# Mean squares of a gated norm on one NeuronCore: four transposes and a column sum in place of eight products with a column of ones

## The chip, the cores and the metric

One core of a Trainium2 chip runs the whole kernel in one launch. The metric is the device time in microseconds (us) of one execution. The engines are PE (TensorE), whose weight loads are listed apart as PEld, DVE (VectorE), ACT (ScalarE), POOL (GpSimd) and SP (SyncE), which issues the transfers.

## What is computed

Input x has 32 sequences of 64 tokens with 512 features, 2048 tokens in all. Three sublayers are added to it in turn, each on the layer norm of what came before: a state space layer, an attention of 32 heads over a small context, and a mixture of four low-rank experts. Nearly all of the time is in the first, which in short is:

```
proj = input_states @ in_proj_w.T           # gate 8192, x 8192, B and C 1024 each, dt 128
xBC  = silu(conv(xBC) + conv_b)             # 4 taps, causal, per channel
y    = _ssd(hs, A, Bm, Cm, D, dt, dt_bias)  # decayed attention inside each sequence
g    = y * silu(gate)
gg   = g.reshape(b, l, G, GS)               # G = 8 groups of GS = 1024 channels
var  = mean(gg * gg, axis=-1)               # one number for each token and group
g    = gg * rsqrt(var + EPS) * norm_w
out  = g @ out_w.T
```

The change concerns `var`: for each token, the mean of 1024 squares.

## The kernel before

The tokens are cut into 4 blocks of 512 (`TB`) and the channels into 8 groups. An iteration is one block and one group, 32 iterations in all (`number(tb, g)`), and their loops are unrolled. Each engine has its own list of instructions, written out by hand in the order in which it runs them. Semaphores join the lists: a `wait_ge` holds back everything behind it on its engine.

In an iteration channels lie on the partitions and the block's 512 tokens along the columns. A group's input weights are 18 units of 128 channels: B, C, and eight pairs X and G. Each unit is 12 products of 128x512 on PE (`unit`, into the PSUM banks `p_in`), since weights and activations are split in two parts of type fp32r and three combinations of the parts are added up. DVE and ACT run the convolution (`conv`). X tiles are transposed on PE (`to_tokens`: four transposes of 128x128, as products of `x_t` and the identity `id_sb`). The decayed attention is `heads`, products of 64x64 into the two PSUM banks of `p_y`. DVE multiplies with the gate (`gated`, the tile `g_f`). ACT rounds that to `g_hi` and squares it to `g_sq`, and POOL makes the rest `g_lo` and adds the squares of the eight channel tiles into `ss` (128 channels by 512 tokens, fp32). The output projection (`project`) adds 12 products for each channel tile into the four banks `p_out`.

`rsqrt(var + EPS)` is the same for all channels of a group, so it is applied after the projection: `accumulate` multiplies each `p_out` tile, in which tokens are on the partitions, with the column `rms`. For this the mean squares are wanted with the tokens on the partitions. `mean_squares` on PE does that: for each of the four token tiles, `ss` is the stationary operand and a column of ones the moving one, so that the product is the sum over channels, one column of `p_y[:, 1, :]`. Each such fp32 product runs as two weight loads and two matmuls, so a call has eight. DVE's `variance` scales the four columns and adds 1e-5 (`msv`), POOL's `inverse_rms` raises them to the power -0.5 (`rms`).

The place: the mean squares of iteration n - 1 are made in iteration n, behind its units 4 and 5 and in front of half of a projection:

```python
unit(5, tb, g, n)
mean_squares(n - 1)
project(CPG - 1, *back, range(0, 2))
slot(1, tb, g, n)
to_tokens(1, n)
```

`slot(1)` begins with PE's wait for `msv_done`, since PE is about to write `p_y` again (in some iterations at once, with four transposes of expert rows, `experts_in`, or of step sizes, `by_token`; in the others later). On DVE, `variance(n - 1)` stands behind the convolution of unit 4 and in front of `x_tokens(1)`, which waits for `to_tokens(1)`. On POOL, `inverse_rms(n - 1)` comes a little later, in front of `g_low(0, n)`.

The last iteration's mean squares are made behind the loop by code of their own, with ones.

Of the kernel before, what the change touches and what calls it, by code (L numbers as in the profile page):

```python
# [7 lines left out]
P = 128  # L8
# [6 lines left out]
CPG = INTER // GROUPS // P  # L15
# [3 lines left out]
QT = TB // P  # L19
ITERS = NTB * GROUPS  # L20
# [18 lines left out]
def decoder_kernel(nc, x, ctxv, amask, wt, wdt, owt, params, dtb, alog, ffa, ffb,  # L39
                   ident, c_mask, c_bd, c_v2, c_eq, out):  # L40
    F32, F32R = mybir.dt.float32, mybir.dt.float32r
    ACT, ALU, AX = mybir.ActivationFunctionType, mybir.AluOpType, mybir.AxisListType
# [7 lines left out]
    with outer:  # L50
        def alloc(stack):
            def sb(name, shape, dt=F32, align=None):
                wide = 4 * int(np.prod(shape[1:])) >= 256
                return stack.enter_context(nc.sbuf_tensor(name, shape, dt, align_bytes=align or (64 if wide else 32)))
            return sb

        def sem(name):
            return outer.enter_context(nc.semaphore(name))

        sb = alloc(outer)  # L60
        id_sb = sb("id_sb", [P, P])
        half_neg = sb("half_neg", [P, QT])
        ones = sb("ones", [P, 1])
# [7 lines left out]
        dpar = sb("dpar", [P, CPG])  # L71
        dts = sb("dts", [P, QT, HPG])
        msv = sb("msv", [P, QT])
        rms = sb("rms", [P, QT])
        st6 = sb("st6", [P, QT, 6])
        mv = sb("mv", [P, QT, 2])
# [11 lines left out]
        p_y = outer.enter_context(nc.psum_tensor("p_y", [P, 2, 512], F32))  # L88
# [4 lines left out]
        sb = alloc(main)  # L93
# [4 lines left out]
        sb = alloc(loop)  # L98
# [16 lines left out]
        ss = sb("ss", [P, TB])  # L115
# [22 lines left out]
        sb = alloc(raw)  # L138
# [11 lines left out]
        sb = alloc(tail)  # L150
# [21 lines left out]
        s_done = sem("s_done"); tr_done = sem("tr_done"); xtok_done = sem("xtok_done")  # L172
        y_done = sem("y_done"); yread = sem("yread"); g_done = sem("g_done")
        sq_done = sem("sq_done"); ghi_done = sem("ghi_done"); glo_done = sem("glo_done"); ss_done = sem("ss_done")
        out_done = sem("out_done"); ms_done = sem("ms_done"); msv_done = sem("msv_done"); rms_done = sem("rms_done")
        dve_own = sem("dve_own"); act_own = sem("act_own"); tap_own = sem("tap_own"); ln_own = sem("ln_own")
        dif_first = sem("dif_first"); clamp_first = sem("clamp_first"); exp_first = sem("exp_first"); s_first = sem("s_first")
        first_in = [sem(f"first_in{h}") for h in range(2)]
# [63 lines left out]
        def waves(stage, places):  # L242

            turns = [(at, q, k) for k, ats in places.items() for q, at in enumerate(ats) if at is not None]
            for _, q, k in sorted(turns):
                y0, y1 = TAIL_BANKS[q]
                stage(k, q, LOOP_TILES + q, tail_tiles[q], y0, y1)
# [222 lines left out]
        def _(pe):  # L470
            def mm(o, l, r, first, last):
                return nc.tensor.matmul(o, lhsT=l, rhs=r, start=first, stop=last)  # L472
# [320 lines left out]
            def mean_squares(n):  # L793
                pe.wait_ge(ss_done, SUMS * (n + 1))
                pe.wait_ge(yread, CPG * (n + 1))
                pe.sem_inc(hold, 1)
                for h in range(QT):
                    tok = slice(h * P, (h + 1) * P)
                    ins = mm(p_y[:, 1, h:h + 1], ss[:, tok], ones[:, :], True, True)
                ins.then_inc(ms_done, 1)  # L800

            def body(tb, g):
# [14 lines left out]
                if begun:  # L817
                    state_products(n)
                    project(CPG - 2, *back)
                    to_tokens(0, n)  # L820

                    unit(4, tb, g, n)
# [5 lines that stand above are left out]
                else:  # L828
                    unit(4, tb, g, n)
                    unit(5, tb, g, n)  # L830
                    pe.wait_ge(dtr_done, 1)
                    by_token(0)
                    state_products(n)
                    to_tokens(0, n)
                    unit(6, tb, g, n, 1)
# [31 lines left out]
            for h in range(QT):  # L867
                tok = slice(h * P, (h + 1) * P)
                mm(p_y[:, 1, h:h + 1], ss[:, tok], ones[:, :], True, False)
                mm(p_y[:, 1, h:h + 1], g_sq[:, 0, tok], ones[:, :], False, False)  # L870
                ins = mm(p_y[:, 1, h:h + 1], g_sq[:, 1, tok], ones[:, :], False, True)
# [3 lines left out]
            c = CPG - 1  # L875
            pe.wait_ge(o_ld[c % RING_O], 16 * ((CPG // RING_O) * (ITERS - 1 - GROUPS) + c // RING_O + 1))
            pe.wait_ge(glo_done, CPG * ITERS)
            for h in range(QT):
                tok = slice(h * P, (h + 1) * P)
                for j, (ga, wo) in enumerate(((g_hi, 0), (g_hi, 1), (g_lo, 0))):  # L880
                    ins = mm(p_out[h][:, :], ga[:, c % 2, tok], o_ring[:, c % RING_O, wo, :], False, j == 2)
# [415 lines left out]
        def _(dve):  # L1297
            V = nc.vector
# [185 lines left out]
            def gated(c, n):  # L1484

                dve.wait_ge(yread, CPG * n + c + 1)
                dve.wait_ge(gate_done, CPG * n + c + 1)
                if c >= 2 or not first(n):
                    dve.wait_ge(sq_done, CPG * n + c - 1)
                    dve.wait_ge(glo_done, CPG * n + c - 1)  # L1490
                V.tensor_tensor(g_f[:, c % 2, :], t_y[:, c % 2, :], sg[:, (CPG * n + c) % GATES, :], ALU.mult).then_inc(g_done, 1)  # L1491

            def variance(n):
                dve.wait_ge(ms_done, n + 1)
                V.tensor_scalar(msv[:, :], p_y[:, 1, 0:QT], 1.0 / (CPG * P), 1e-5, ALU.mult, ALU.add).then_inc(msv_done, 1)

            def accumulate(tb, n):
# [184 lines left out]
            def body(tb, g):  # L1682
# [51 lines left out]
                for k in range(1 if begun else 2, CPG):  # L1734
# [8 lines left out]
                    if k == 1 and begun:  # L1743
                        variance(n - 1)
# [33 lines left out]
            for c in (CPG - 2, CPG - 1):  # L1778
                skipped(c, ITERS - 1)
                gated(c, ITERS - 1)  # L1780
            variance(ITERS - 1)

            def moments_and_mean(S, src):

# [288 lines left out]
```

## Time and profile before

| | us |
|---|---|
| median of 3 runs (2845.37 to 2847.9) | 2847.12 |
| the profiled execution's own time | 2843.42 |
| its span, from first to last instruction | 2841.6 |

| engine | busy us | share of the span |
|---|---|---|
| PE | 2804.8 | 99% |
| PEld | 2274.4 | 80% |
| DVE | 1990.1 | 70% |
| ACT | 1462.6 | 51% |
| POOL | 1315.5 | 46% |

The rows further down come from one profiled execution, whose time is 3.7 us below the median of the runs. Times in a row are us from the start of the span unless they are marked ns. A matmul's end is modelled, and matmuls overlap, so that the busy time of PE is no sum of costs: what a piece of PE work costs is read from the chain of work, or from one start to the next. The mean granted clock of TensorE over the span is 0.997 of full speed.

### The profile page before, as it was taken

The numbers are of one execution on the slowest core, as the hardware profiler recorded it, in microseconds if no ns is written. First come the engines' busy times: TensorE is split into PE (matmuls) and PEld (weight loads), VectorE is DVE, ScalarE is ACT, GpSimd is POOL, SyncE is SP. The second block draws the span as 40 slices with busy tenths as digits, with TensorE's granted clock in tenths as the row PEclk, the third lists the DMA queues.
The fourth block names the chain that finished last, engine by engine and source line by source line (L and its number), as shares of the span: only waits on it lengthen the run. The fifth ranks groups of instructions, "written<-read, shape, count | busy, mean of one in ns | idle before, by whom it ended". The sixth has DMA issues, their size and how long they took to land.

```text
span 2841.6 us, 56494 instructions
## 1 busy us (share of the span) xinstructions
PE 2804.8 (99%) x22298; PEld 2274.4 (80%) x22298; DVE 1990.1 (70%) x3152; ACT 1462.6 (51%) x2205; POOL 1315.5 (46%) x840
## 2 busy tenths in 40 slices
PE   7999999999999999999999999999999999999998
PEld 5788888878788788887888888888888888878886
DVE  8777768887667757677676766677666666666767
ACT  5666656655445545445445454544545444453545
POOL 4766767775344333443343443424434334343334
PEclk9999999999999999999999999999999999999999
DMA  7788777778565555565665665555656656555530
GB/s 253 274 298 300 264 270 258 269 257 291 181 200 189 181 183 182 181 192 182 203 193 180 200 189 174 186 180 185 203 180 192 193 173 203 181 184 187 186 130 31
DMA packets 179428, 578.27 MB, mean 203 GB/s; under 512 B 25248, under 2 KB 31904, under 8 KB 171104
## 3 DMA queue, kind: packets, MB, share of 16 engines
q1 hardware_dynamic: 179168, 574.66, 61.5%
q8 instruction: 180, 2.95, 0.4%
q14 instruction: 80, 0.66, 0.1%
HBM read 460.29 MB, written 114.29 MB: 202 GB/s over the span
## 4 chain that ended last, share of the span: by engine, by line
PE 91%; DVE 6%; ACT 1%; issue 1%; DMA 0%; POOL 0%; SPq 0%; DVEq 0%; ACTq 0%; POOLq 0%
PE p_in L472 53%; PE p_out L472 23%; PE p_y L472 9%; PE p_in L562 4%; DVE cv L1430 1%; PE p_y L700 1%; DVE o_ring L1370 1%; DVE t_y L1479 0%; DVE g_f L1491 0%; DVE mx L1600 0%; ACT cv L942 0%; DVE sc L1587 0%; DVE cum L1392 0%; DMA raw_w<-wt 0%; DVE decay L1462 0%
## 5 line engine op out<-in xcount | busy, mean ns | idle before, releaser
L472 PE MATMUL p_in<-xnb,w_ring 128*128 128x512 f32 x6864 | 1673.2, 396 | 1.8 <-DVE cv L1430 0.9
L472 PEld LDWEIGHTS p_in<-xnb,w_ring 128*128 128x128 f32 x6864 | 1260.8, 188 | 262.6 <-issue 2.7
L1430 DVE SCALAR_TENSOR_TENSOR cv<-p_in,cpar,cv 128x504 f32<-128x504 f32 x954 | 699.8, 734 | 469.2 <-ACT cv L942 445.4
L1856 POOL TENSOR_TENSOR g_lo<-g_f,g_hi 128x512 fp32r<-128x512 f32 x256 | 338.1, 1322 | 1195.8 <-ACT g_hi L942 1195.8
L472 PE MATMUL p_out<-o_ring,g_hi 128*128 128x512 f32 x2048 | 638.3, 393 | 1.7 <-POOL g_lo L1856 1.7
L942 ACT ACTIVATE cv<-p_in,cpar 128x512 f32<-128x512 f32 x318 | 246.6, 775 | 636.9 <-PE p_in L472 600.5
L472 PEld LDWEIGHTS p_out<-o_ring,g_hi 128*128 128x128 f32 x2048 | 379.4, 188 | 80.3 <-issue 2.3
L472 PE MATMUL p_out<-o_ring,g_lo 128*128 128x512 f32 x1024 | 399.6, 390 | 0.0
L1467 DVE TENSOR_TENSOR x_tok<-p_in,dts 128x512 f32<-128x512 f32 x256 | 176.5, 689 | 285.7 <-PE p_in L562 284.0
L942 ACT ACTIVATE x_t<-cv 128x512 f32<-128x512 f32 x256 | 160.9, 628 | 309.9 <-DVE t_y L1479 285.9
L1867 POOL TENSOR_TENSOR ss<-ss,g_sq 128x512 f32<-128x512 f32 x190 | 310.3, 1633 | 7.4
L1911 POOL TENSOR_TENSOR decay<-decay,cumk 128x2048 f32<-128x2048 f32 x63 | 234.8, 3727 | 38.9 <-DMA decay<-cum_scr 37.7
L942 ACT ACT_TABLE_LOAD x183 | 234.8, 1283 | 4.0 <-PEq L2067 0.7
L1848 POOL TENSOR_TENSOR w_ring<-raw_w,w_ring 128x512 fp32r<-128x512 f32 x144 | 209.2, 1477 | 51.5 <-ACT w_ring L942 35.8
L942 ACT ACTIVATE sg<-p_in 128x512 f32<-128x512 f32 x254 | 149.3, 588 | 160.9 <-PE p_in L472 160.9
L472 PEld LDWEIGHTS p_out<-o_ring,g_lo 128*128 128x128 f32 x1024 | 192.2, 188 | 40.7
L1479 DVE SCALAR_TENSOR_TENSOR t_y<-x_t,dpar,p_y 128x256 f32<-128x256 f32 x512 | 210.9, 474 | 1.1 <-PE p_y L472 1.1
L1491 DVE TENSOR_TENSOR g_f<-t_y,sg 128x512 f32<-128x512 f32 x256 | 180.2, 744 | 0.1
L942 ACT ACTIVATE g_hi<-g_f 128x512 fp32r<-128x512 f32 x256 | 159.2, 623 | 32.8 <-DVE g_f L1491 32.3
L472 PEld LDWEIGHTS p_y<-decay,x_tok 64*64 64x64 f32 x8192 | 131.1, 134 | 46.2 <-issue 46.2
L562 PE MATMUL p_in<-id_sb,x_t 128*128 128x128 f32 x1024 | 158.7, 278 | 7.1 <-ACT x_t L942 5.2
L562 PEld LDWEIGHTS p_in<-id_sb,x_t 128*128 128x128 f32 x1024 | 118.2, 141 | 51.5 <-issue 20.6
(258 smaller groups left out, 2251.4 us busy)
## 6 DMA issues: line engine op xcount, KB each, us to landing
w_ring<-ws_scr SPq DMA_DIRECT2D x432, 512.0 KB, 3.7
o_ring<-ows_scr SPq DMA_DIRECT2D x192, 512.0 KB, 4.6
ws_scr<-w_ring SPq DMA_DIRECT2D x144, 512.0 KB, 5.9
decay<-cum_scr SPq DMA_DIRECT2D x126, 512.0 KB, 6.7
raw_w<-wt SPq DMA_DIRECT2D x144, 256.0 KB, 5.1
ows_scr<-o_ring SPq DMA_DIRECT2D x64, 512.0 KB, 6.3
raw_o<-owt SPq DMA_DIRECT2D x64, 256.5 KB, 5.6
acb<-x SPq DMA_DIRECT2D x3, 1024.0 KB, 7.7
```

What stands on the lines that cost most here:

```text
L472: return nc.tensor.matmul(o, lhsT=l, rhs=r, start=first, stop=last)
L562: ins = nc.tensor.transpose(p_in[1][:, q * P:(q + 1) * P], x_t[:, c % 2, q * P:(q + 1) * P], id_sb[:, :])
L700: ins = nc.tensor.transpose(banks[rl][:, gp * P:(gp + 1) * P], pv, id_sb[:, :])
L942: return nc.scalar.activation(dst, src, func, **kw)
L1430: ins = V.scalar_tensor_tensor(acc[:, :, t:SEQ], src[:, :, 0:SEQ - t], cpar[:, 5 * m + 3 - t:5 * m + 4 - t], acc[:, :, t:SEQ], ALU.mult, A ...
L1467: V.tensor_tensor(x_tok[:, c % 2, :, :].rearrange("p q (h d) -> p q h d", h=2), p_in[1][:, :].rearrange("p (q h d) -> p q h d", q=QT, h=2) ...
L1479: ins = V.scalar_tensor_tensor(t_y[:, c % 2, :].rearrange(by_seq, q=QT, s=2)[:, s], x_t[:, c % 2, :].rearrange(by_seq, q=QT, s=2)[:, s], d ...
L1491: V.tensor_tensor(g_f[:, c % 2, :], t_y[:, c % 2, :], sg[:, (CPG * n + c) % GATES, :], ALU.mult).then_inc(g_done, 1)
L1848: T(w_ring[:, k % RING_W, 1, :, :].rearrange("p k c -> p (k c)"), raw_w[:, (UNITS * g + k) % RAW_W, :], w_ring[:, k % RING_W, 0, :, :].rea ...
L1856: T(g_lo[:, c % 2, :], g_f[:, c % 2, :], g_hi[:, c % 2, :].bitcast(F32), ALU.subtract).then_inc(glo_done, 1)
L1867: T(ss[:, :], a, g_sq[:, c % 2, :], ALU.add).then_inc(ss_done, 1)
L1911: T(decay[:, blk, :, :, :], decay[:, blk, :, :, :], last.unsqueeze(3).broadcast_to([P, 8, QT, SEQ]), ALU.subtract) \
```

## The change

`mean_squares` now transposes the four 128x128 tiles of `ss` into the whole bank `p_y[:, 1, :]`: tokens on the partitions, 128 channels along the columns for each of the four token tiles. `variance` on DVE then sums each group of 128 columns with a tensor_reduce into a new tile `mst`, waits for its own result with a new semaphore `mst_own`, and scales as before, from `mst`. The call behind the loop keeps its products with ones, and a `last_variance` with the old form. So 31 calls change.

```diff
@@ -796,7 +797,7 @@
                 pe.sem_inc(hold, 1)
                 for h in range(QT):
                     tok = slice(h * P, (h + 1) * P)
-                    ins = mm(p_y[:, 1, h:h + 1], ss[:, tok], ones[:, :], True, True)
+                    ins = nc.tensor.transpose(p_y[:, 1, tok], ss[:, tok], id_sb[:, :])
                 ins.then_inc(ms_done, 1)
@@ -1492,6 +1493,12 @@
             def variance(n):
                 dve.wait_ge(ms_done, n + 1)
+                V.tensor_reduce(mst[:, :], p_y[:, 1, :].rearrange("p (h c) -> p h c", h=QT), AX.X, ALU.add).then_inc(mst_own, 1)
+                dve.wait_ge(mst_own, n + 1)
+                V.tensor_scalar(msv[:, :], mst[:, :], 1.0 / (CPG * P), 1e-5, ALU.mult, ALU.add).then_inc(msv_done, 1)
+
+            def last_variance(n):
+                dve.wait_ge(ms_done, n + 1)
                 V.tensor_scalar(msv[:, :], p_y[:, 1, 0:QT], 1.0 / (CPG * P), 1e-5, ALU.mult, ALU.add).then_inc(msv_done, 1)
@@ -1778,7 +1785,7 @@
-            variance(ITERS - 1)
+            last_variance(ITERS - 1)
```

PE's list in the second iteration, from the transposes of x's first tile to the next units, before (a product with ones is one row entry here, and two matmuls on the chip):

```order
L562 MATMUL p_in<-id_sb,x_t 128x128 x4
L472 MATMUL p_in<-xnb,w_ring 128x512 x24
L472 MATMUL p_y<-ones,ss 128x1 x4
L472 MATMUL p_out<-o_ring,g_hi 128x512 x2
L472 MATMUL p_out<-o_ring,g_lo 128x512
L472 MATMUL p_out<-o_ring,g_hi 128x512 x2
L472 MATMUL p_out<-o_ring,g_lo 128x512
L562 MATMUL p_in<-id_sb,x_t 128x128 x4
L472 MATMUL p_in<-xnb,w_ring 128x512 x12
```

and in the changed kernel, where lines are numbered one higher:

```order
L563 MATMUL p_in<-id_sb,x_t 128x128 x4
L473 MATMUL p_in<-xnb,w_ring 128x512 x24
L800 MATMUL p_y<-id_sb,ss 128x128 x4
L473 MATMUL p_out<-o_ring,g_hi 128x512 x2
L473 MATMUL p_out<-o_ring,g_lo 128x512
L473 MATMUL p_out<-o_ring,g_hi 128x512 x2
L473 MATMUL p_out<-o_ring,g_lo 128x512
L563 MATMUL p_in<-id_sb,x_t 128x128 x4
L473 MATMUL p_in<-xnb,w_ring 128x512 x12
```

Nothing on PE changes its place; only the third row differs.

DVE's list at the same place, before (the three rows of `cv` are the convolution of unit 4):

```order
L1430 SCALAR_TENSOR_TENSOR cv<-p_in,cpar,cv 128x8x63
L1430 SCALAR_TENSOR_TENSOR cv<-p_in,cpar,cv 128x8x62
L1430 SCALAR_TENSOR_TENSOR cv<-p_in,cpar,cv 128x8x61
L1495 TENSOR_SCALAR msv<-p_y 128x4
L1467 TENSOR_TENSOR x_tok<-p_in,dts 128x512
```

and in the changed kernel:

```order
L1431 SCALAR_TENSOR_TENSOR cv<-p_in,cpar,cv 128x8x63
L1431 SCALAR_TENSOR_TENSOR cv<-p_in,cpar,cv 128x8x62
L1431 SCALAR_TENSOR_TENSOR cv<-p_in,cpar,cv 128x8x61
L1496 TENSOR_REDUCE mst<-p_y 128x4
L1498 TENSOR_SCALAR msv<-mst 128x4
L1468 TENSOR_TENSOR x_tok<-p_in,dts 128x512
```

DVE has one instruction more between the convolution and the multiplication of the transposed x.

## Rows read from the trace of the kernel before

**Rows 1.** The page: busy time by engine, and the chain that ended last.

```profile
PE 2804.8 (99%) x22298; PEld 2274.4 (80%) x22298; DVE 1990.1 (70%) x3152; ACT 1462.6 (51%) x2205; POOL 1315.5 (46%) x840
...
PE 91%; DVE 6%; ACT 1%; issue 1%; DMA 0%; POOL 0%; SPq 0%; DVEq 0%; ACTq 0%; POOLq 0%
```

**Rows 2.** Two stretches: length, busy of each engine (instructions), clock, DMA share, GB/s.

```profile
100.00:800.00 700.00, 696.09 (x5286) 565.77 (x5285) 524.67 (x741) 405.74 (x629) 460.69 (x284) 1.00 0.77 262
800.00:2700.00 1900.00, 1898.99 (x15199) 1543.46 (x15198) 1286.51 (x2078) 928.00 (x1362) 740.75 (x465) 1.00 0.58 187
```

**Rows 3.** Chain of work, one iteration: start, us on the chain, engine, tile, line, matmuls.

```profile
212.80 0.79 PE p_y L472 x8
213.58 1.51 PE p_out L472 x6
...
222.32 1.36 PE p_out L472 x6
223.68 0.48 PE p_in L562 x4
224.16 5.49 PE p_in L472 x24
...
251.41 0.44 PE p_in L562 x4
251.85 2.78 PE p_in L472 x12
...
280.03 5.44 PE p_in L472 x24
```

**Rows 4.** Weight loads by form: line, tiles, shape, count, busy us, mean ns.

```profile
L562 PEld LDWEIGHTS p_in<-id_sb,x_t 128*128 128x128 f32 x1024 | 118.2, 141 | 51.5 <-issue 20.6 <-ACT x_t L942 14.2 <-DVE t_y L1479 3.2
L472 PEld LDWEIGHTS p_y<-ones,ss 128*128 128x128 f32 x256 | 33.6, 191 | 2.9 <-issue 0.5
```

**Rows 5.** Timeline at one call: start, us, engine, line, operation.

```profile
884.59 0.72 DVE L1430 SCALAR_TENSOR_TENSOR cv<-p_in,cpar,cv 128x488 f32<-128x488 f32 x1
884.68 0.95 PE L472 MATMUL p_y<-ones,ss 128*128 128x1 f32 x8
885.67 0.16 DVE L1495 TENSOR_SCALAR msv<-p_y 128x4 f32<-128x4 f32 x1 [0.35 <-PE p_y L472]
...
886.98 0.60 PE L732 MATMUL p_y<-id_sb,row_l 128*128 128x128 f32 x4
887.41 0.60 PE L562 MATMUL p_in<-id_sb,x_t 128*128 128x128 f32 x4
...
888.05 0.69 DVE L1467 TENSOR_TENSOR x_tok<-p_in,dts 128x512 f32<-128x512 f32 x1 [2.22 <-PE p_in L562]
```

**Rows 6.** DVE by form: count, busy us, mean ns, idle before.

```profile
L1600 DVE TENSOR_REDUCE mx_l<-sc_l 128x16 f32<-128x1024 f32 x24 | 28.1, 1212 | 0.0
L1607 DVE TENSOR_REDUCE sm_l<-sc_l 128x32 f32<-128x2048 f32 x12 | 27.3, 2276 | 0.0
L1640 DVE TENSOR_TENSOR x2s_l<-row_l,acb 128x512 f32<-128x512 f32 x12 | 8.2, 684 | 0.0
L1680 DVE SCALAR_TENSOR_TENSOR x2s_l<-p_y,x2s_l 128x512 f32<-128x512 f32 x12 | 8.2, 680 | 0.0
```

**Rows 7.** Timeline of a place where PE waited for ACT.

```profile
86.23 0.63 ACT L942 ACTIVATE x_t<-cv 128x512 f32<-128x512 f32 x1 [0.34 <-DVE cv L1430]
86.91 0.66 PE L562 MATMUL p_in<-id_sb,x_t 128*128 128x128 f32 x4 [1.30 <-ACT x_t L942]
```

**Rows 8.** Timeline of a place where PE waited for DVE.

```profile
735.97 0.68 DVE L1343 TENSOR_TENSOR xnb<-p_y,xnb 128x512 fp32r<-128x512 f32 x1
...
736.91 0.81 PE L472 MATMUL p_y<-decay,x_tok 64*64 64x64 f32 x39 [0.51 <-DVE xnb L1343]
```

**Rows 9.** Timeline of POOL behind one call: start, us, what, idle before.

```profile
885.91 1.02 POOL L1871 TENSOR_TENSOR rms<-msv,half_neg 128x4 f32<-128x4 f32 x1 [0.41 <-DVE msv L1495]
896.81 1.30 POOL L1856 TENSOR_TENSOR g_lo<-g_f,g_hi 128x512 fp32r<-128x512 f32 x1 [9.88 <-ACT g_hi L942]
```

More of the change, by code:

```diff
@@ L73, in decoder_kernel @@
         msv = sb("msv", [P, QT])
+        mst = sb("mst", [P, QT])
         rms = sb("rms", [P, QT])
@@ L174, in decoder_kernel @@
         sq_done = sem("sq_done"); ghi_done = sem("ghi_done"); glo_done = sem("glo_done"); ss_done = sem("ss_done")
-        out_done = sem("out_done"); ms_done = sem("ms_done"); msv_done = sem("msv_done"); rms_done = sem("rms_done")
+        out_done = sem("out_done"); ms_done = sem("ms_done"); mst_own = sem("mst_own"); msv_done = sem("msv_done"); rms_done = sem("rms_done")
         dve_own = sem("dve_own"); act_own = sem("act_own"); tap_own = sem("tap_own"); ln_own = sem("ln_own")
```

## The prediction

> **What bounds the kernel now.** I read the page first: PE is busy for 99% of the span and makes 91% of the chain that ended last, DVE is busy for 70% [rows 1]. Since the busy time of PE counts overlapping matmuls, I then read two stretches of the loop: from 100 to 800 us PE lacks 3.9 us of being busy all the time, from 800 to 2700 only 1.0 us in 1900 [rows 2]. So in 31 iterations hardly anything but PE's own list sets the end, and time taken out of that list shortens the kernel one for one, as long as no other engine makes PE wait instead. DVE, ACT and POOL have room as averages; whether DVE has it at the place of the change is a question of a few tenths of a microsecond and is worked out below. The granted clock is 1.00 in both stretches, the higher of its two levels (2.4 GHz).
>
> **What PE loses.** The chain of work tells what a piece costs PE when it is packed between other matmuls. The eight matmuls with ones take 0.79 us, and the six of the projection behind them take 1.51 us, where six elsewhere take 1.36 [rows 3]. The second difference belongs to the cost: something of the switch from these short products back to the wide ones is paid in the first of them. So a call costs 0.79 + 0.15 = 0.94 us.
>
> **What PE gains in work.** The trace has four transposes of the same shape and type in 256 places, those of `x_t`. One group takes 0.48 us on the chain, and the 24 matmuls behind it 5.49 where 24 elsewhere take 5.44: 0.53 us. Another takes 0.44, with 2.78 for the 12 behind it, where twice 1.36 = 2.72 would be the plain time: 0.50 us [rows 3]. I take 0.51. What stands behind the new transposes is the same projection as now, whose start behind transposes the trace does not show; the p_in units behind `x_t` are products of the same size and type, and I use them.
>
> The saving is 0.94 - 0.51 = 0.43 us a call, and 31 x 0.43 = 13.3 us. The bounds: without the terms for what stands behind, 0.79 - 0.44 = 0.35 us, 10.9 us in all; with the penalty of 0.15 charged to the ones and none to the transposes, 0.94 - 0.44 = 0.50 us, 15.5 us.
>
> Why four transposes are cheaper than eight matmuls of one column each can be seen from the weight loads. There are 1024 loads for the 32 x 8 x 4 transposes, so one each, and 256 for the 32 x 4 products with ones, so two each [rows 4]. Both load 128x128. On the chain a product with ones takes 0.79 / 8 = 0.10 us and a transpose 0.44 / 4 = 0.11 us: a load is paid, not the columns that stream.
>
> The Trainium skill has a rule that speaks against the change and one that speaks for it, both in "TensorE: Matmul & The Clock Gate", sections "Back-to-back issue gap" and "LDWEIGHTS (loading the stationary operand)". By the first, a matmul of 1 to 64 columns takes about 60 cycles, with a floor of about 25 ns, and one of 128 columns 134: eight short ones would cost less than four transposes. By the second a load takes its 128 columns at 1.2 GHz, 107 ns, whatever the matmul streams: an estimate of 0.85 us for eight and 0.43 us for four. The trace's 0.79 and 0.44 us agree with the second.
>
> **What DVE gains in work, and whether PE waits for it.** Each call adds a tensor_reduce of 128x512 to 128x4, from PSUM. The trace has reduces of 1024 columns at 1212 ns and of 2048 at 2276 ns, both from SBUF [rows 6]: 1.04 ns a column with about 148 ns on top, so 0.68 us for 512. An operation of 512 columns takes 680 ns with an operand in PSUM and 684 ns without, so that the source should not matter [rows 6]. The scaling behind it stays at 0.16 us [rows 5], and between the two lies the wait for the own result, for which I take 0.04 us, about what lies between ACT's end and PE's start in [rows 7] (0.05).
>
> Now the place, in the clock of one call [rows 5]. The matmuls with ones start at 884.68. The convolution in front of `variance` ends at 884.59 + 0.72 = 885.31. DVE got the transposes of `x_t` 888.05 - 887.41 = 0.64 us after their first start, so the new ones would be there at 884.68 + 0.64 = 885.32: the two arrive together. Then the reduce ends at about 886.01, and `msv` at 886.01 + 0.04 + 0.16 = 886.21, instead of 885.83 now.
>
> Who waits for `msv`? PE does, in `slot(1)`, with everything behind it on its list. The next work there starts now at 886.98, and with 0.43 us saved would start at 886.55. From the end of an awaited instruction to PE's start the trace shows 86.91 - 86.86 = 0.05 us at the shortest [rows 7] and 736.91 - 736.65 = 0.26 at the longest of such waits in the loop [rows 8]. So PE could start at 886.26 to 886.47, before 886.55. I take the stall as nothing. The cover is the half projection, six matmuls of some 1.4 us, and what is left of it is 0.08 to 0.29 us. It is thin: beyond it each 0.1 us on the path through DVE costs 31 x 0.1 = 3.1 us.
>
> DVE itself loses nothing by it: `x_tok` waits 2.22 us for PE at this place [rows 5], more than the 0.38 us by which `msv` is later plus the 0.43 us by which PE comes earlier. POOL gets `msv` 0.38 us later where it waits for it, and then has 9.88 us of idle time in front of its next `g_lo` [rows 9]; `rms` is wanted only by `accumulate`, which stands on DVE's list behind the next unit's convolution and four more steps. No transfer depends on any of it, and the memory of `ss` comes free for POOL's next sums earlier, not later. The code behind the loop is as before.
>
> **Where some of it may go again.** From 100 to 800 us PE has 3.9 us of waits for ACT and DVE, one such at 735.97 [rows 2, 8]. Where a wait stands behind the change in the same iteration and the other engine isn't driven by PE, the gain is lost there: at most some four iterations of the 31, 4 x 0.43 = 1.7 us, at least nothing. I take 0.8. Sum: 13.3 - 0.8 = 12.5 us. The profiled execution at 2843.4 us would go to 2830.9, and the median of the runs, 3.7 us above it, from 2847.1 to 2834.6.
>
> **The rivals.**
>
> The thin cover is used up. If the reduce cost the 1.21 us of the row with 1024 columns (two passes, or a slower read of PSUM), `msv` would end at 886.74 and PE start at 886.79 to 887.00, 0.24 to 0.45 us late: what is left is 0.19 us a call at best and nothing at worst, so 2841 to 2847 us. For it: no reduce in the trace reads PSUM. Against it: no row of DVE shows a price for PSUM. 12 in 100.
>
> Slower than before, by the same mechanism at full size: the place is DVE's reduce, PE stands in `slot(1)`. If it cost what the row of 2048 columns shows, 2.28 us, `msv` ends at 887.81, PE starts at about 888.0, 1.4 us late, and loses 1.4 - 0.43 = 1.0 us a call: 31 us, 2878. It decides from a reduce of 0.68 + 0.2 + 0.43 = 1.3 us for no gain, and of about 1.5 us for a loss above 0.2%. Nothing in the rows speaks for so much. 4 in 100. The page "VectorE: DVE Perf Modes" of the Trainium skill, section "Rules for kernel authors", calls tensor_reduce VectorE's slowest operation on a hot path and expects its 1x rate; the 1.04 ns a column above are that, and no more.
>
> The transposes are paid by their columns. Four of 128 columns are one of 512, 5.44 / 24 = 0.23 us, and short products would be nearly free, if `p_y`'s 16 to 64 small products were the measure; then the change adds 0.1 us at most to each call, 31 x 0.1 = 3 us, 2850. Against it stand the 0.94 us that the ones cost now and the 0.44 us of the other transposes. The first of the two rules quoted from the Trainium skill would give this. 3 in 100.
>
> The gain is taken out of PE but PE waits for others by as much (ACT's `x_t`, DVE's convolution), everywhere and not only in the first block. Against it: from 800 to 2700 us PE waits 1.0 us in 22 iterations, and DVE is idle for 32% of that stretch [rows 2]. 2845 us or so, 3 in 100. That the change does not do what it says, eight matmuls to four, I leave within this one, since the counts of the loads bear it out.
>
> **How the numbers follow.** The forecast, 0.35 to 0.50 us a call with up to 1.7 us lost again, is worth 78 in 100: a gain of 9.2 to 15.5 us, 2831.6 to 2837.9, and about 2 us more to both sides for the spread of the runs. The range of 8 in 10 takes in part of the used-up cover: 2829 to 2842. A measurement of this kernel can tell about 0.2%, 5.7 us, from no change. Faster by more than that: 78 and a third of the 12, 82. Within it: the rest of the 12, the columns and the lost gain, 14. Slower: 4.
>
> **What would show it.** In the changed profile the chain should have the transposes of `ss` at 0.44 to 0.48 us and the six matmuls behind at 1.36 to 1.42. The reduce should take 0.68 us and start within 0.05 us of the convolution's end; `msv` should end some 0.4 us later than now, counted from the first matmul of the call; and PE should have no waits for `msv` in its list of waits, or only tenths in all. The time from one call to the next should be shorter by 0.43 us. The prediction is wrong if the reduce takes over 0.9 us, if PE waits for `msv` each time, or if the projection behind the transposes starts as late as it does behind the ones.

## The result: slower by 0.9%

| | before | changed |
|---|---|---|
| median, us | 2846.24 (4 runs, 2842.27 to 2847.9) | 2870.69 (4 runs, 2868.22 to 2873.22) |
| profiled execution, us | 2843.42 | 2870.57 |
| span, us | 2841.6 | 2868.8 |

The ratio is 1.0089, with a 95% interval of 1.0076 to 1.0102: 24 us slower, where 12.5 us faster was forecast.

The page of the changed kernel, busy time by engine and the shares of the chain, against [rows 1]:

```profile
PE 2799.8 (98%) x22174; PEld 2262.5 (79%) x22174; DVE 2048.6 (71%) x3183; ACT 1462.2 (51%) x2205; POOL 1309.2 (46%) x840
...
PE 91%; DVE 5%; issue 2%; ACT 1%; DMA 0%; POOL 0%; SPq 0%; DVEq 0%; POOLq 0%; ACTq 0%
```

PE has its 124 matmuls less (22298 to 22174), and 5 us less busy time. DVE's busy time grew by 58.5 us. 31 reduces of 0.69 us make 21.4 of it. One small instruction grew by 39.8 us in its 31 executions, and a few other rows lost some 2.7. By tile `mst`, with the shortest, median and longest duration in ns:

```profile
L1496 DVE TENSOR_REDUCE mst<-p_y x31: 681/692/692, 133.4 to 2736.8; 128x4 f32<-128x512 f32 x31
L1498 DVE TENSOR_SCALAR msv<-mst x31: 170/1755/2518, 134.1 to 2737.6; 128x4 f32<-128x4 f32 x31
```

The reduce is as forecast. The scaling of four columns, 0.16 us before [rows 5], takes 0.17 us at the shortest, 1.75 in the median and 2.52 at the longest.

PE's stretches, against [rows 2] (length, busy of PE, PEld, DVE, ACT, POOL, clock, DMA share, GB/s):

```profile
100.00:800.00 700.00, 687.91 (x5222) 556.11 (x5222) 536.90 (x742) 405.95 (x629) 454.74 (x282) 1.00 0.77 261
800.00:2700.00 1900.00, 1877.18 (x14942) 1520.67 (x14941) 1312.89 (x2079) 914.53 (x1342) 735.53 (x463) 1.00 0.58 185
```

PE lacks 12.1 and 22.8 us of being busy, where it lacked 3.9 and 1.0: it waits. The clock is the same, 1.00. The list of PE's waits (us in total, times, longest) puts most of that down to "issue", which means that the profile found no releaser. That it is the scaling shows in the ends: in each of the 19 calls with a long wait PE starts 0.10 us after the scaling has ended. The rows:

```profile
PE p_in L563 <- issue: 26.1, 16, 2.0
...
PE p_y L501 <- issue: 5.3, 3, 2.0
...
PE p_in L563 <- DVE msv L1498: 1.7, 1, 1.7
```

These are 20 waits, 33.1 us in all; the kernel before had one wait of 0.2 us in these three kinds.

One call in order of time, of the seven in the first block that look like it:

```profile
381.58 3.68 POOL L1918 TENSOR_TENSOR decay<-decay,cumk 128x2048 f32<-128x2048 f32 x1
...
382.17 0.60 PE L800 MATMUL p_y<-id_sb,ss 128*128 128x128 f32 x4
...
382.81 0.69 DVE L1496 TENSOR_REDUCE mst<-p_y 128x4 f32<-128x512 f32 x1
...
383.53 1.76 DVE L1498 TENSOR_SCALAR msv<-mst 128x4 f32<-128x4 f32 x1
...
385.39 0.63 PE L563 MATMUL p_in<-id_sb,x_t 128*128 128x128 f32 x4 [1.23 <-issue]
```

POOL's subtraction ends at 381.58 + 3.68 = 385.26. The scaling, started at 383.53, ends at 385.29, 0.03 us later, and PE starts 0.10 us after that. The reduce ran beside the same POOL instruction at its usual 0.69 us. Another call, with the POOL instruction begun 0.17 us after the transposes:

```profile
806.58 3.68 POOL L1918 TENSOR_TENSOR decay<-decay,cumk 128x2048 f32<-128x2048 f32 x1
...
807.77 2.52 DVE L1498 TENSOR_SCALAR msv<-mst 128x4 f32<-128x4 f32 x1
...
810.38 0.63 PE L563 MATMUL p_in<-id_sb,x_t 128*128 128x128 f32 x4 [1.99 <-issue]
```

POOL ends at 810.26, the scaling at 810.29. In 19 of the 31 calls POOL's subtraction is running when the scaling starts, and the scaling ends 0.02 to 0.03 us after it. In the other 12 POOL has ended it before, and the scaling takes 0.17 us. PE's next start is due 1.84 us after the first transpose, as it comes where nothing holds it; in the 12 calls it comes at 1.83 or 1.84, in seven of the 19 at 3.2 to 3.7 and in twelve at 3.98. The sum of these delays is 35.8 us.

So the account is 35.8 us lost in 19 calls, against the 13.3 that were to be gained in 31: 22.5 us slower, inside the measured 21.6 to 29.0; some 2 us of the 24 stay unaccounted for.

### The profile page after: what moved, and what is told of

It is laid out like the page before. It is cut to its first block, busy times and chain, and to the rows that moved or that the text cites. A ratio compares the mean times of both kernels' runs of the same rounds, so it can differ in the third digit from the quotient of the medians.

```text
span 2868.8 us, 56277 instructions
## 1 busy us (share of the span) xinstructions
PE 2799.8 (98%) x22174; PEld 2262.5 (79%) x22174; DVE 2048.6 (71%) x3183; ACT 1462.2 (51%) x2205; POOL 1309.2 (46%) x840
## 4 chain that ended last, share of the span: by engine, by line
PE 91%; DVE 5%; issue 2%; ACT 1%; DMA 0%; POOL 0%; SPq 0%; DVEq 0%; POOLq 0%; ACTq 0%
PE p_in L473 53%; PE p_out L473 23%; PE p_y L473 8%; PE p_in L563 4%; DVE cv L1431 1%; PE p_y L701 1%; DVE o_ring L1371 1%; PE p_y L800 0%; DVE t_y L1480 0%; DVE cum L1393 0%; DVE mx L1607 0%; DVE sc L1594 0%; DMA raw_w<-wt 0%; ACT cv L943 0%; DVE decay L1463 0%
## 5 line engine op out<-in xcount | busy, mean ns | idle before, releaser
L943 ACT ACTIVATE g_hi<-g_f 128x512 fp32r<-128x512 f32 x256 | 159.2, 623 | 33.1 <-DVE g_f L1492 32.6
```

The lines of the kernel that those rows point to most:

```text
L943: return nc.scalar.activation(dst, src, func, **kw)
```

## Experiments

The theory (theory 1 in the texts on record): a DVE instruction of a certain kind can't run while POOL works on SBUF, but ends when POOL's instruction does; the scaling became of this kind when its source moved from PSUM to SBUF. The rivals: the two-step chain with its own wait, or the reduce, or the transposes are slow in themselves, and POOL is a coincidence.

The comparisons below are with the kernel before, run again on the same chip (medians of 2843.6 to 2846.4 us). How many us a run is faster or slower is given by the medians and by the ratio, where the two differ. In the diffs `....` stands for the rest of an expression. Unless another is named, they are against the changed kernel.

**e1_sums_in_psum**: the same instructions, but the sums are kept in PSUM.

```diff
-V.tensor_reduce(mst[:, :], p_y[:, 1, :]....then_inc(mst_own, 1)
+V.tensor_reduce(p_y[:, 0, 0:QT], p_y[:, 1, :]....then_inc(mst_own, 1)
 dve.wait_ge(mst_own, n + 1)
-V.tensor_scalar(msv[:, :], mst[:, :], 1.0 / (CPG * P), 1e-5, ALU.mult, ALU.add)
+V.tensor_scalar(msv[:, :], p_y[:, 0, 0:QT], 1.0 / (CPG * P), 1e-5, ALU.mult, ALU.add)
```

> The changed kernel, but the reduce writes its four sums to PSUM (four columns of the other bank of p_y, free at that moment), and the scaling reads them there; same instructions, same waits. Theory 1, POOL holds the way to SBUF that the scaling wants when it reads SBUF and writes SBUF: the scaling takes 0.16 to 0.17 us in all 31 calls, PE starts behind the half projection 1.84 us after the first transpose in all calls, and the gain forecast for PE's list appears: 12 to 14 us under the kernel before, some 2833 us. Theory 2, the chain of two steps with its own wait is slow in itself, or POOL's work slows whatever DVE runs beside it: the scaling stays at 1.8 to 2.5 us in 19 calls and the time at about 2870.

Measured: 2832.13 us against 2843.58, ratio 0.9956 (0.9944 to 0.9968), 11 to 13 us faster than before. The scaling by line, shortest, median and longest in ns:

```profile
L1498 DVE TENSOR_SCALAR msv<-p_y x31: 160/161/163, 133.5 to 2697.6; 128x4 f32<-128x4 f32 x31
```

and one call, with POOL's subtraction running over all of it:

```profile
376.55 3.69 POOL L1918 TENSOR_TENSOR decay<-decay,cumk 128x2048 f32<-128x2048 f32 x1
...
377.15 0.60 PE L800 MATMUL p_y<-id_sb,ss 128*128 128x128 f32 x4
...
377.50 0.72 PE L473 MATMUL p_out<-o_ring,g_hi 128*128 128x512 f32 x2
...
377.78 0.70 DVE L1496 TENSOR_REDUCE p_y<-p_y 128x4 f32<-128x512 f32 x1
...
378.52 0.16 DVE L1498 TENSOR_SCALAR msv<-p_y 128x4 f32<-128x4 f32 x1
...
378.99 0.60 PE L563 MATMUL p_in<-id_sb,x_t 128*128 128x128 f32 x4
```

The scaling is 0.16 us in all 31 calls, and PE starts 378.99 - 377.15 = 1.84 us after the first transpose. The own wait, the reduce and the transposes are cleared by this: all of them are still there. The place of the sums is the whole difference of 1.3%, and this version beats both kernels.

**e2_ones_two_steps**: the products with ones as before and no reduce, only the scaling in two steps through SBUF. The diff is against the kernel before.

```diff
 ins = mm(p_y[:, 1, h:h + 1], ss[:, tok], ones[:, :], True, True)
...
-V.tensor_scalar(msv[:, :], p_y[:, 1, 0:QT], 1.0 / (CPG * P), 1e-5, ALU.mult, ALU.add)
+V.tensor_scalar(mst[:, :], p_y[:, 1, 0:QT], 1.0 / (CPG * P), None, ALU.mult).then_inc(mst_own, 1)
+dve.wait_ge(mst_own, n + 1)
+V.tensor_scalar(msv[:, :], mst[:, :], 1e-5, None, ALU.add)
```

> The eight products with ones as before, no transposes and no sum over columns; only the scaling is in two steps through the SBUF tile mst (times 1/1024 from PSUM, then plus 1e-5 from SBUF to SBUF). Theory 1: the second step ends with POOL's subtraction wherever that is running. From the trace of before, POOL's subtraction ends 3.09 to 3.54 us after the first product in seven calls and 3.86 in twelve, and PE's next work is due at 2.30, so PE is late by 0.9 to 1.4 and by 1.7 us: 27 us in all, about 2873. Theory 2a, the price is in the reduce or the transposes: within 1 us of before, 2846. Theory 2b, an own wait costs a microsecond or more in itself: also slower, but in all 31 calls alike.

Measured: 2869.24 us, ratio 1.0093 (1.0078 to 1.0107), 26 us slower; 27 were worked out from the trace of before by laying the step over POOL's subtractions. The two steps:

```profile
L1496 DVE TENSOR_SCALAR mst<-p_y x31: 161/162/164, 132.9 to 2736.3; 128x4 f32<-128x4 f32 x31
L1498 DVE TENSOR_SCALAR msv<-mst x31: 169/1935/2705, 133.1 to 2736.5; 128x4 f32<-128x4 f32 x31
```

The same kind of operation on the same four columns is held when it reads SBUF and not when it reads PSUM, in one kernel. One four-column instruction, with nothing else of the change, costs as much as the whole change lost.

**e3_transposes_no_sum**: PE's part alone; the scaling reads four columns of the transposed bank, and the sum over channels is left out.

```diff
-V.tensor_reduce(mst[:, :], p_y[:, 1, :]....then_inc(mst_own, 1)
-dve.wait_ge(mst_own, n + 1)
-V.tensor_scalar(msv[:, :], mst[:, :], 1.0 / (CPG * P), 1e-5, ALU.mult, ALU.add)
+V.tensor_scalar(msv[:, :], p_y[:, 1, 0:QT], 1.0 / (CPG * P), 1e-5, ALU.mult, ALU.add)
```

> The four transposes, but no sum over columns: the scaling reads the first four columns of the transposed bank from PSUM, so that the mean squares are wrong. It measures PE's part alone. Both theories: the saving on PE's list, 0.35 to 0.50 us a call, 11 to 15 us under before, 2831 to 2835, with no wait of PE for msv. If it is slower than before, the transposes themselves are at fault and both theories fall.

Measured: 2831.52 us, ratio 0.9954 (0.9941 to 0.9968): 12 to 13 us faster. The transposes give what was forecast for them, and e1 with its reduce gives as much, so the reduce costs nothing that can be measured.

**e4_short_pool**: the changed kernel as it is, with less work on POOL at the moment in question: the second subtraction of each iteration is done for one of its eight heads and left out for seven.

```diff
+if blk == 1:
+    T(decay[:, blk, 0:1, :, :], decay[:, blk, 0:1, :, :], last[:, 0:1, :]....broadcast_to([P, 1, QT, SEQ]), ALU.subtract)
+    return
```

> The changed kernel as it is, scaling from SBUF to SBUF, but POOL's subtraction for the second half of the heads (the instruction that runs beside the scaling) is cut to one of its eight heads; the other seven are left unsubtracted, so the output is another. The instruction should go from 3.7 us to about 0.5. Theory 1: with nothing running on POOL at that moment the scaling takes 0.17 to 0.3 us in nearly all calls and the time falls to 2830 to 2840. Theory 2: POOL does not matter, and it stays at about 2870.

Measured: 2828.49 us, ratio 0.9946 (0.9931 to 0.9960), 15 us faster than before; the intervals of this ratio and of e1's overlap. POOL's instruction went from 3.7 to 0.62 us in the median (0.61 to 0.80), and it has ended in all 31 calls when the scaling starts. The scaling from SBUF to SBUF:

```profile
L1498 DVE TENSOR_SCALAR msv<-mst x31: 169/169/170, 133.6 to 2696.4; 128x4 f32<-128x4 f32 x31
```

The same instruction as in the changed kernel is never held once POOL is out of its way. With e1 and e2 this shows both halves of the condition for a tensor_scalar: it needs POOL working, and a source in SBUF.

**e5_sum_twice**: e1 with the reduce done twice, to measure how much time the half projection covers. The diff is against e1, whose wait for `n + 1` it replaces by the two waits.

```diff
+V.tensor_reduce(p_y[:, 0, 0:QT], p_y[:, 1, :]....then_inc(mst_own, 1)
+dve.wait_ge(mst_own, 2 * n + 1)
 V.tensor_reduce(p_y[:, 0, 0:QT], p_y[:, 1, :]....then_inc(mst_own, 1)
+dve.wait_ge(mst_own, 2 * n + 2)
```

> As e1_sums_in_psum, with the sum over columns done twice, each followed by the wait for the own result. It measures the cover. One more reduce and wait, 0.69 + 0.04 us, puts the end of msv 2.26 us behind the first transpose; PE's next work is due at 1.84. Theory 1: PE is late by 0.4 to 0.55 us in every call, 31 x 0.4 to 0.55 = 12 to 17 us above e1, so the gain is just used up: 2843 to 2849, and each tenth of a microsecond beyond the cover costs 3.1 us. If the cover were larger than the prediction made it (0.08 to 0.29 us), the time would stay under 2840.

Measured: 2846.51 us, ratio 1.0005 (0.9996 to 1.0015). A call of it:

```profile
377.43 0.60 PE L800 MATMUL p_y<-id_sb,ss 128*128 128x128 f32 x4
...
378.07 0.70 DVE L1496 TENSOR_REDUCE p_y<-p_y 128x4 f32<-128x512 f32 x1
...
378.80 0.70 DVE L1498 TENSOR_REDUCE p_y<-p_y 128x4 f32<-128x512 f32 x1
...
379.53 0.16 DVE L1500 TENSOR_SCALAR msv<-p_y 128x4 f32<-128x4 f32 x1
...
379.80 0.63 PE L563 MATMUL p_in<-id_sb,x_t 128*128 128x128 f32 x4 [0.37 <-issue]
```

The second reduce adds 0.73 us to the path and takes the gain back to nothing. PE goes on 379.80 - 377.43 = 2.37 us behind the first transpose instead of 1.84. It is 0.53 us late, as in 27 of the 31 calls, and 0.7 to 0.8 us in the other four. So 0.20 us of the 0.73 were covered, and the rest was paid in full. The whole times say the same within their intervals: against e1 the ratios differ by 0.0049, 14 us or 0.45 us a call. In e1 PE starts 0.30 us after the scaling's end and here 0.10 us after it, which is the same 0.20. The forecast had 0.08 to 0.29 us of cover left.

**e6_two_inputs**: the changed kernel, with another kind of instruction for the scaling. `epsb` is a new SBUF tile filled with 1e-5.

```diff
-V.tensor_scalar(msv[:, :], mst[:, :], 1.0 / (CPG * P), 1e-5, ALU.mult, ALU.add)
+V.scalar_tensor_tensor(msv[:, :], mst[:, :], 1.0 / (CPG * P), epsb[:, :], ALU.mult, ALU.add)
```

> The changed kernel, sums in SBUF, but the scaling is a scalar_tensor_tensor of two SBUF tiles (the sums, and a tile filled with 1e-5) in place of a tensor_scalar of one. It asks what in the scaling wants what POOL holds. If it is only the mode in which DVE runs a tensor_scalar from SBUF to SBUF, the step takes 0.16 to 0.2 us and the time is 2830 to 2836. If a second SBUF input wants it too, the step is held until POOL's subtraction ends, as in the changed kernel: about 2870.

Measured: 2869.61 us, ratio 1.0083 (1.0068 to 1.0098).

```profile
L1500 DVE SCALAR_TENSOR_TENSOR msv<-mst,epsb x31: 161/1740/2507, 132.0 to 2735.7; 128x4 f32<-128x4 f32 x31
```

Held just as long. So it isn't something of tensor_scalar alone: an instruction with two inputs in SBUF is held too, until 0.02 us after POOL's subtraction.

**e7_wait_for_sums**: the changed kernel with one word changed on PE, whose wait is now for the sums.

```diff
 if k == 1:
     pe.wait_ge(cbt_done, n + 1)
     if not first(n):
-        pe.wait_ge(msv_done, n)
+        pe.wait_ge(mst_own, n)
```

> The changed kernel as it is, scaling from SBUF to SBUF, but PE's wait in slot(1) is for the sums (mst_own) instead of the scaled values (msv_done): the bank p_y has been read by then. The scaling should still take 1.8 to 2.5 us in 19 calls. Theory 1 says that this alone costs nothing, and that the loss is PE standing behind it: PE starts 1.84 us behind the first transpose everywhere, and DVE, held until 3.9 us after it, still has x_tok ready for PE at about 4.7 us, when heads want it at about 4.9: 2830 to 2838. If a held DVE costs PE time further on, the time stays well above 2840.

Measured: 2833.34 us, ratio 0.9957 (0.9942 to 0.9973). The scaling is still held, and PE no longer stands behind it:

```profile
797.53 3.69 POOL L1918 TENSOR_TENSOR decay<-decay,cumk 128x2048 f32<-128x2048 f32 x1
...
798.73 2.52 DVE L1498 TENSOR_SCALAR msv<-mst 128x4 f32<-128x4 f32 x1
...
799.21 0.60 PE L563 MATMUL p_in<-id_sb,x_t 128*128 128x128 f32 x4
...
801.17 0.68 DVE L1468 TENSOR_TENSOR x_tok<-p_in,dts 128x512 f32<-128x512 f32 x1
```

The held instruction costs nothing by itself; PE's wait for it was the whole loss. DVE makes `x_tok` directly behind it, 801.17 - 799.21 = 1.96 us after the start of the transposes of `x_t` instead of 0.63, and the gain of e1 is there all the same.

**e8_copy_by_reduce**: e1, and then a copy from SBUF to SBUF by an operation with one input that is not a tensor_scalar. The diff is against e1.

```diff
-V.tensor_scalar(msv[:, :], p_y[:, 0, 0:QT], 1.0 / (CPG * P), 1e-5, ALU.mult, ALU.add)
+V.tensor_scalar(mst[:, :], p_y[:, 0, 0:QT], 1.0 / (CPG * P), 1e-5, ALU.mult, ALU.add).then_inc(mst_own, 1)
+dve.wait_ge(mst_own, 2 * n + 2)
+V.tensor_reduce(msv[:, :], mst[:, :].unsqueeze(2), AX.X, ALU.add)
```

> Sums in PSUM as in e1_sums_in_psum, scaled from there into SBUF (mst), and then one step more from SBUF to SBUF: msv is a tensor_reduce of mst over one element, a copy with a single SBUF input in an operation other than tensor_scalar. It asks whether any DVE instruction that reads SBUF is held while POOL works. If only a tensor_scalar from SBUF to SBUF and an operation with two SBUF inputs are held, the copy takes 0.16 us, msv ends 1.7 us behind the first transpose, just before PE's 1.84, and the time is 2832 to 2837. If every SBUF input is held, the copy takes up to 2.4 us and the time is about 2870.

Measured: 2830.56 us, ratio 0.9953 (0.9936 to 0.9971).

```profile
L1500 DVE TENSOR_REDUCE msv<-mst x31: 156/157/158, 132.4 to 2697.5; 128x4 f32<-128x4 f32 x31
```

Not held. So reading SBUF beside POOL does not hold every DVE instruction. The runs sort small DVE instructions by what happens to them beside POOL's subtraction: held are a tensor_scalar from SBUF to SBUF, and an operation with two SBUF inputs; free are the tensor_scalar from PSUM and the reduce with one input, in PSUM or in SBUF.

This is what the Trainium skill says in "SBUF — State Buffer", section "Who interferes with whom": VectorE and GpSimd share one pair of SBUF ports, whoever holds it has it for a whole instruction, and the other is fully blocked. By that section VectorE needs the pair for a tensor_scalar from SBUF to SBUF in its two-port mode, or for a second SBUF input while GpSimd's instruction reads SBUF (the subtraction does), and not for a tensor_reduce. All of e1, e2, e4, e6 and e8 agree, down to four columns: a scaling of 0.17 us waits for the rest of a 3.68 us subtraction. What the runs show is which instructions are held and until when. The ports and the mode themselves are seen in no trace here.

## Why the prediction was wrong

**What bounds the kernel**: right. PE's list is shorter by 0.45 us a call, 14 us in all, and e3 measured 12 to 13 (9 to 17 by its interval).

**PE's saving, 0.43 us a call**: right in size. In e1 the chain of work has the call thus:

```profile
213.94 0.44 PE p_y L800 x4
214.38 1.40 PE p_out L473 x6
```

That is 0.44 + 0.04 us where 0.51 was taken, against the 0.94 of the ones [rows 3]: 0.46 us, 14.3 in all. From one start to the next it is the same: PE's next start comes 2.29 us behind the first product with ones, and 1.84 us behind the first transpose. e1 measured 11 to 13, e3 12 to 13, with intervals of some 9 to 17. Whether the small remainder is the 0.8 us that was set aside for gains lost at other waits can't be told apart from the spread of the runs.

**The reduce, 0.68 us, starting as the convolution ends**: right, 0.69 us.

**"The scaling behind it stays at 0.16 us"**: this is the step that failed. The row behind it [rows 5] was the scaling as it stood, from PSUM. The change moved its source to SBUF, and I carried the duration over as if only the number of columns mattered. The prediction's "the source should not matter" came from two rows of 512 columns [rows 6], 680 ns with an operand in PSUM and 684 ns with both in SBUF. Only one of those 24 executions ran beside a POOL instruction, and it had its operand in PSUM, so the rows could not show the difference. The duration of 0.16 us held in 12 calls, in which POOL's subtraction had happened to end before; in 19 the scaling was held until POOL's subtraction ended, and ran up to 2.5 us. Everything after it followed as the prediction had it: PE stands in `slot(1)`, the cover is 0.20 us, and what exceeds it is paid in full.

The trace of before had shown this for the same kind of instruction on another tile. By tile `gates_l`, a tensor_scalar of four columns from SBUF to SBUF (shortest, median, longest in ns):

```profile
L1654 DVE TENSOR_SCALAR gates_l<-mid_l,lmax_l x12: 231/1352/1361, 915.3 to 2786.6; 128x4 f32<-128x4 f32 x12
```

and by tile `row_l`, two tensor_scalars of the same 512 columns:

```profile
L1580 DVE TENSOR_SCALAR row_l<-acb,mv_l,rd_l x12: 537/541/546, 736.6 to 2646.0; 128x512 f32<-128x512 f32 x12
...
L1647 DVE TENSOR_SCALAR row_l<-x2s_l,mv_l,rd_l x12: 547/1374/1377, 880.1 to 2770.5; 128x512 f32<-128x512 f32 x12
```

A small operation whose median is six times its shortest is held by something, and the timeline names it:

```profile
915.31 1.36 DVE L1654 TENSOR_SCALAR gates_l<-mid_l,lmax_l 128x4 f32<-128x4 f32 x1
915.35 1.29 POOL L1856 TENSOR_TENSOR g_lo<-g_f,g_hi 128x512 fp32r<-128x512 f32 x1 [7.23 <-ACT g_hi L942]
```

In 11 of the 12 executions it ends 0.02 to 0.03 us after this instruction of POOL, though POOL's starts 0.04 us after it. PE's list of waits names none of these rows, so they did not stand out. And the timeline of before had POOL at work at the very place:

```profile
376.33 3.69 POOL L1911 TENSOR_TENSOR decay<-decay,cumk 128x2048 f32<-128x2048 f32 x1
```

It ends at 380.02, 3.10 us after the products with ones begin, where PE wants to go on at 2.29. Laid side by side the two give the loss: e2's expectation, worked out from this trace alone once the rule was suspected, was 27 us, and e2 measured 26.

**The rivals.** The one that ended slower had the right place and the right way of paying (PE in `slot(1)`, DVE too late for the cover), at 31 us, but hung it on the reduce, whose price was well known, and gave it 4 in 100. It asked how long an instruction takes, and not what else runs beside it. The transposes priced by their columns fell with e3; a gain lost to other waits fell with e3 as well.

**What depended on `msv` otherwise**: right. POOL's power and `accumulate` have room for microseconds; e7, where only PE is let off, gets the whole gain.

## What to carry to other kernels

When a change moves the source of a small tensor_scalar on DVE from PSUM to SBUF, or gives a DVE instruction a second SBUF input, look on POOL's timeline for what runs at that moment: the instruction may end only when POOL's does. Its own duration from another place is worth something only if the shortest, median and longest of its form agree. If a third engine waits for the result, keep the small values in PSUM (e1), or let that engine wait for the last thing that it really needs (e7): either one turned a loss of 0.9% into a gain of 0.4%.

## What was not expected of the hardware

A DVE instruction of four columns can take 2.52 us instead of 0.17, for as long as a POOL instruction of another tile lasts. That is the case above. Two smaller things concern what PE's work costs.

The whole saving lies in the group of small products itself. Eight matmuls with ones take 885.49 - 884.68 = 0.81 us, from their first start to the first start of the projection behind them:

```profile
885.49 0.72 PE L472 MATMUL p_out<-o_ring,g_hi 128*128 128x512 f32 x2
```

Four transposes take 377.50 - 377.15 = 0.35 us (the call of e1 above). The six products behind them take 1.48 us to PE's next start in both kernels. In most places where the six stand behind wide products they take 1.38. So the 0.10 us of going over to wide products is paid behind the transposes as well. The chain of work has it as 0.15 and 0.04 us, because it counts from modelled ends; its sums, 0.94 and 0.48 us, hold.

The list of waits and the chain show a wait shorter than it is. The changed kernel's chain at the call of 382 us:

```profile
384.17 1.23 issue
385.39 0.63 PE p_in L563 x4
```

Without the wait the chain gives the group 0.44 us [rows 3]. From one start to the next, PE is 3.22 - 1.84 = 1.38 us late, and from the first transpose to the next unit it takes 0.38 us, where it takes 0.35 in the same call of e1. The stall costs 1.41 us, and hardly any of that is a dearer group. The rest of the difference is that the wait is counted from the modelled end of the product in front, and in a packed list the next one starts 0.16 us before that end. With 0.16 us added to each of the 19 long waits, the 33 us of the list become the 36 of the starts.
